# GNN node stage on one core: ScalarE's transposed-x1 and h1 copies placed between two halves of the four output-row activations

## The reference

```
h1 = relu(x @ W_self0 + b0)
x1 = layernorm(x + h1 @ W_self1 + b1)              # layer 0, no neighbours
v  = x1 @ Wskip + bskip                            # layer 1, no edges
lin = layernorm(v) * ln_g + ln_b  ->  @ Wlin + blin
out = layernorm(x1 + elu(lin + x1))
```

## Time and profile before

| | |
|---|---|
| median of 3 runs | 1772.49 us (1771.62 to 1773.52) |
| profiled execution | 1765.38 us, its span 1763.6 us |
| span: busy PE / DVE / ACT / POOL | 86% / 71% / 64% / 59% |
| 200 to 300 us, inside the node stage: PE / DVE / ACT / POOL busy | 94.11 / 97.92 / 92.77 / 81.75 us of 100 |
| the same stretch: granted TensorE clock | 1.00 of full speed |

### The profile page before, as it was taken

How to read it: one execution, slowest core, us unless ns; L and a number is a source line. 1 busy time by engine, 2 the same in 40 slices (tenths; PEclk the granted TensorE clock), 3 DMA queues, 4 the chain that set the end, 5 groups by cost and what they waited for, 6 DMA issues and landing times. The chain is left out here.

```text
span 1763.6 us, 33507 instructions
## 1 busy us (share of the span) xinstructions
PE 1520.7 (86%) x7745; PEld 1065.6 (60%) x7745; DVE 1254.9 (71%) x6050; ACT 1125.1 (64%) x3051; POOL 1044.4 (59%) x1038
## 2 busy tenths in 40 slices
PE   3599999999999998989455469999999999999992
PEld 2477777777777776777345335555555555555541
DVE  4799999999999996545366545666666666666652
ACT  0499999999999994333144415666666666666672
POOL 4688888868888774653576364555454554545220
PEclk9799999999999999999666699999999999999995
DMA  2366666644444442332121221111111111111000
GB/s 78 108 154 160 154 159 154 156 150 143 148 142 149 141 144 68 84 83 64 30 55 54 58 62 35 38 39 40 38 39 40 38 39 38 40 39 39 15 13 4
DMA packets 124685, 142.48 MB, mean 81 GB/s; under 512 B 32654, under 2 KB 75625, under 8 KB 124574
## 3 DMA queue, kind: packets, MB, share of 16 engines
q1 hardware_dynamic: 97374, 105.01, 19.8%
q0 software_dynamic: 27200, 36.26, 9.0%
HBM read 75.35 MB, written 74.38 MB: 85 GB/s over the span
## 5 line engine op out<-in xcount | busy, mean ns | idle before, releaser
L1227 POOL DMA_INDIRECT out_dram<-big,idx x98 | 99.1, 1011 | 298.4 <-ACT big L1396 159.5
L1210 POOL DMA_INDIRECT big<-x_tab,look x196 | 199.5, 1018 | 92.4 <-issue 61.5
L683 PE MATMUL pb<-MG_s,big 128*128 128x256 f32 x832 | 207.4, 392 | 39.5 <-issue 25.0
L683 PEld LDWEIGHTS pb<-MG_s,big 128*128 128x128 f32 x832 | 149.5, 189 | 141.7 <-issue 79.6
L708 ACT ACTIVATE big<-big 128x128 f32<-128x128 f32 x416 | 170.1, 481 | 0.0
L803 POOL TENSOR_TENSOR big<-big,cl 128x512 f32<-128x512 f32 x104 | 133.3, 1281 | 48.7 <-ACT big L732 41.0
L665 PE MATMUL pb<-C_s,big 128*128 128x128 f32 x832 | 161.9, 276 | 0.0
L666 PE MATMUL pb<-Ws1c_s,big 128*128 128x128 f32 x832 | 161.8, 276 | 0.0
L317 POOL DMA_INDIRECT a_xs<-in_x_dram,idx x98 | 98.8, 1008 | 93.3 <-issue 48.5
L1537 DVE CUSTOM_DVE_ANT_0 big<-pb,big,zero 128x128 f32<-128x128 f32 x392 | 113.9, 346 | 54.2 <-PE pb L1299 53.0
L1038 POOL DMA_INDIRECT big<-h1e_tab,hidx x98 | 102.7, 1048 | 75.1 <-POOLq L1628 33.3
(11 more groups left out here) (339 smaller groups left out, 4016.2 us busy)
## 6 DMA issues: line engine op xcount, KB each, us to landing
big<-in_x_dram SPq DMA_DIRECT2D x104, 256.0 KB
x_tab<-big SPq DMA_DIRECT2D x98, 256.0 KB
out_dram<-big SPq DMA_DIRECT2D x98, 256.0 KB
h1e_tab<-a_rows SPq DMA_DIRECT2D x25, 256.0 KB
x_tab<-a_rows SPq DMA_DIRECT2D x25, 256.0 KB
big<-in_edge_attr_dram SPq DMA_DIRECT2D x97, 64.0 KB
big<-x_tab,look POOLq DMA_INDIRECT x196
dst_row<-in_dst_dram POOLq DMA_DIRECT2D x13, 240.2 KB
```

Source lines behind the costliest of these rows:

```text
L683: t = pe.matmul(o, b_x1T[:, r * P:(r + 1) * P], MG_s[:], start=True, stop=True)
L1210: g.indirect_dma_start(out=o, out_offset=None, in_=x1_tab, in_offset=bass.IndirectOffsetOnAxis(ap=look[:, a, j:j + 1], axis=0), bounds_che ...
```

## The change

ScalarE's four output rows of a turn are no longer issued in one piece. Two are, then come the copy of transposed x1 and the copy of h1, then the other two rows. The waits stand with the instructions that they stood with. The semaphore `b_o` is raised by the last row, as before.

```diff
+        def rows_out(act, u, r):
+            return act.activation(b_o[u % 2][:, r * D:(r + 1) * D], b_w[u % 2][:, r * D:(r + 1) * D],
+                                  ACT.Identity, scale=brs3[:, r:r + 1], bias=b_nm3[:, r:r + 1])
...
                     act.wait_ge(step("b_nm3"), made(B_LAG, "b_nm3", it, 6))
                     act.wait_ge(dma_st[(u - 2) % 4], landed(i + (1 if u >= 2 else 0)))
-                    for r in range(R):
-                        t = act.activation(b_o[u % 2][:, r * D:(r + 1) * D], b_w[u % 2][:, r * D:(r + 1) * D],
-                                           ACT.Identity, scale=brs3[:, r:r + 1], bias=b_nm3[:, r:r + 1])
-                    t.then_inc(step("b_o"), 1)
+                    for r in range(R // 2):
+                        rows_out(act, u, r)
...
                     act.activation(b_h1T, PH[:], ACT.Relu, bias=b0x[:, 0:1]).then_inc(step("b_h1"), 1)
+
+                    for r in range(R // 2, R):
+                        t = rows_out(act, u, r)
+                    t.then_inc(step("b_o"), 1)
```

## The result

The changed kernel takes 1760.68 us (median of 4, 1760.05 to 1762.55) against 1773.01 us for the kernel before (median of 4, 1771.62 to 1773.59). The ratio is 0.9933, with an interval of 0.9916 to 0.9951: faster by 12.3 us in the medians. The forecast was 1763.5 us, in a range of 1760.5 to 1769.5.

A forecast was written before the change was run, and what follows sets the result against it. Node stage bound by a closed loop of PE and ACT, 5.83 us a turn, holding DVE at 5.857; DVE's own 5.755 next. 100 turns gain 10.2, less 1.2 for collisions: 1772.5 - 9.0 = 1763.5 us, range 1760.5 to 1769.5.

The forecast's parts named there:

- The loop of PE and ACT: Node stage: ACT's copies and PE's transposes and products wait for each other, 5.83 us a turn, falling to 5.06.
- DVE's 5.755: Node stage: DVE's own turn in us, read from two early turns with PE ahead of it, expected as the new limit.
- The collisions: Node stage: DVE's clamp stands still behind POOL's addition, 1.0 us lost at 594.84 in the kernel before; 1.2 us allowed.
- The margin of 0.12: Node stage, early turns: POOL's addition ends 0.12 us before DVE's clamp starts, so they do not collide.
- the rival: Node stage: POOL's addition meets DVE's clamp in every fourth turn, costing 25 us, total 1787; chance 0.03.
- The pair of PE and ACT over two turns: Node stage: loop through PE, 6.18 us, then ACT, 5.21; together 11.39, one turn 5.70, tightest limit under DVE's.
- ACT's own turn: Node stage: ACT alone needs 5.66 us a turn, 5.69 with the split, at most 5.76; an upper figure.
- The late b_o: Node stage: DVE's sum into b_w must wait for rows three and four; loop about 5.2 us, slack 0.55.
- A wait of 0.1 to 0.2 before the logarithm: Node stage, profile after: ACT waits about 0.1 to 0.2 us for DVE's aggregations before the logarithm.
- The split: Node stage, ACT: dividing the four output rows around the copies costs 0.03 us, between nothing and 0.1.
- The profiled execution: Whole kernel: the execution profiled after the change should take near 1756 us, against 1765.38 before.
- 9.0 us off the median: Whole kernel: the node stage's gain is taken off the median 1772.5 us, as later phases just move forward.

The follow-up runs named there:

- e6: Kernel before, with the statistics of b_w reading only the first 64 of 128 features: 1730.63 us, 1.0002 of the kernel before.
- e2: Changed kernel, but only the copy of transposed x1 moved and h1 left behind the fourth row: 1722.71 us, 0.9945 of the kernel before.
- e5: Changed kernel, but three output rows before the two copies and one behind: 1723.20 us, 0.9956 of the kernel before.
- e7: Changed kernel, with the statistics of b_w reading only the first 64 of 128 features: 1710.56 us, 0.9888 of the kernel before.
- e12: Changed kernel with statistics of b_w over 64 of 128 features, run again on another chip: 1746.52 us, 0.9883 of the kernel before.
- e11: Changed kernel with statistics of b_w over 64 of 128 features and without DVE's clamp: 1742.46 us, 0.9864 of the kernel before.
- e3: Changed kernel, but both copies before all four output rows: 1763.61 us, 1.0181 of the kernel before.
- e4: Changed kernel, but one output row before the two copies and three behind: 1725.23 us, 0.9957 of the kernel before.
- e8: Changed kernel, but the last two output rows stand behind the logarithm, so b_o comes later still: 1773.41 us, 1.0242 of the kernel before.
- e9: Changed kernel, unchanged, repeated on another chip: 1755.47 us, 0.9937 of the kernel before.
- e1: Kernel before, run again unchanged: 1731.54 us, 0.9995 of the kernel before.
- e10: Changed kernel without DVE's clamp at zero of the variance of the skip product: 1745.89 us, 0.9879 of the kernel before.

## Why the prediction was right, step by step

- *The loop of PE and ACT bounds the node stage, DVE waits for it 0.10 a turn.* Right: e6 shows a faster DVE to be worth nothing there, e2 that the early copy of x1T alone lifts the limit, e5 that one row less in the loop is enough.
- *The new turn is DVE's 5.755, taken from the early turns.* Right: 576.77 us for 100 turns against a forecast of 575.5 + 1.2 = 576.7. The kernel before shows the figure a second time: the six turns behind its stop at 594.84 take 5.75 to 5.77.
- *The collisions, 1.2 us.* Right in size, 0.24 and 1.0, with the small one of a kind that the rows before did not show after 83 us. But the price of one is not bounded by the 1.0 that was taken for it, as the 1.49 of e7 shows. The margin of 0.12 was the right thing to watch. e7 and e12 show it used up as soon as DVE gets faster, every fourth turn, as the rival had it.
- *The limits under DVE.* The pair of PE and ACT over two turns was named and is the next one, but it was mis-sized: 11.27 in e11 against 11.39, so DVE's margin over it is 0.12 a turn and not 0.06. The part through PE was right (6.22 against 6.18). The part on ACT was too long, because ACT's own turn was taken as 5.83 less the idle 0.17, plus 0.03. It is 5.54 to 5.55. From the last row of x1 to the next first copy ACT needs 0.25 between starts where nothing is waited for, and took 0.55 in the kernel before (median), so ACT waited 0.30 there. The prediction called its figure an upper one.
- *What the prediction did not have.* The loop inside one turn, in which the two copies wait for PE's products behind the copy of xT, stands in the expectations of e3 and e4 (right there within 0.02 us a turn), not among the limits of the prediction. The change stays clear of it by less than 0.2.
- *The late b_o costs nothing.* Right: L775 to L783 is 307.03 - 306.00 = 1.03, before it was 1.06. The rows end at 306.35, some 0.68 before L783. e8 shows what is paid once they are late.
- *A wait of 0.1 to 0.2 before the logarithm.* Right, 0.96 against 0.77.
- *The split costs 0.03.* It costs nothing that shows. Two rows take 304.44 - 303.67 = 0.77 to the copy behind them, as before, and from the copy of h1 to the row behind it are 305.48 - 304.91 = 0.57, where the logarithm stood 303.98 - 303.41 = 0.57 behind it.
- *The profiled execution near 1756.* Wrong: 1760.3. The node stage gave what was forecast, but the later phases of this execution took 3.7 us more than those of the one profiled before. The step that failed is to let the phases behind just move forward, at the precision of single executions.
- *9.0 us off the median.* Measured 12.3 and, in e9, 12.2, where the start of the next phase says 8.8 in the first comparison (for e9 there is no profile of the kernel before on its chip). The first interval just reaches 8.8 us (0.9951), the second takes it in (0.9957). On the two chips with the short later phases e2 and e5, with the same node stage, gained 9.7 and 6.8 us; there the medians and the start of the next phase, against e1 and e6, differ by up to 2.3 us either way (e4 7.1 against 4.9, e3 31.2 against 33.1). Whether some 3 us more are gained in the later phases of the slower chips, or are chance, is open: there is no second profile of the kernel before from a chip with the long ones.

## What to carry to other kernels

This stage, with three engines 93 to 98% busy, was set by a closed loop, and the loop is found by adding starts from wait to wait until the sum is the turn. A short stretch in which another engine happened to run free gave the next limit to the hundredth of a microsecond; the gain is the difference to that, not what was taken out of the loop (here 0.10 of 0.77). An instruction that feeds another engine should be moved up only as far as its own input is ready: with two rows ahead of the copies the kernel gained, with none it lost 31 us.

## What was not expected of the hardware

The phases behind the node stage took 1083 to 1088 us in the first comparison and in e9 to e12, and 1050 to 1055 us in e1 to e8, for the same instructions. In the profile of e1 layer 1's first row sums start at 994.7 us, in that of the kernel before at 1024.6 us, with the node stage within 1 us. Why was not tried.

Removing the clamp also removed its stops without giving new ones. DVE's row sums, statistics and aggregations had ordinary lengths in e10 and e11 while POOL's addition ran. The instructions with both inputs in the tile `big` (L778, L782, L795 there) say little: they never ran together with it in e10, and in e11 only L778 did, twice, over less than 0.12, with no loss. Once, at 649.39, L778 took 0.78 instead of 0.67 beside another instruction of GpSimd (L858, 649.24 to 649.63). So of this turn's work the four-element clamp is the one that was seen to stand behind the addition. The Trainium skill, SBUF — State Buffer, section "Who interferes with whom", names tensor_scalar among the operations that can take the shared pair; the trace agrees, 1.15 us for four elements at 586.86.
